# Perceiver block on one core: rounding the context of the next but one batch on ACT and DVE in place of POOL

## The reference

```python
def _L0_xattn_ref(q, k, v, mask, wq_w, wq_b, wk_w, wk_b, wv_w, wv_b, wo_w, wo_b):
    qh = _split_heads(q @ wq_w.T + wq_b)
    kh = _split_heads(k @ wk_w.T + wk_b)
    vh = _split_heads(v @ wv_w.T + wv_b)
    scores = jnp.einsum('bhqd,bhkd->bhqk', qh, kh) / jnp.sqrt(jnp.float32(D_K))
    scores = jnp.where(mask, scores, jnp.float32(-1000000000.0))
    attn = jax.nn.softmax(scores, axis=-1)
    out = jnp.einsum('bhqk,bhkd->bhqd', attn, vh)
...
x = x + _L0_xattn_ref(_layernorm(x, axis=-1), ctx_1024, ctx_1024, mask_1x1xSxS2_bf1, ...)
```

## Time and profile before

| | |
|---|---|
| median of 3 runs | 1529.22 us (1527.67 to 1531.32) |
| profiled execution: its time | 1530.81 us |
| its span in the profile | 1528.6 us, mean granted TensorE clock 0.992 |
| PE busy | 1470.1 us (96%) |
| DVE busy | 999.5 us (65%) |
| ACT busy | 921.0 us (60%) |
| POOL busy | 447.8 us (29%) |

### The profile page before, as it was taken

One profiled execution on the slowest core, in us unless ns is written; L12 is line 12 of the kernel. 1 busy time (PEld: TensorE's weight loads), 2 busy tenths in 40 slices (PEclk: granted clock), 3 DMA queues, 4 the chain that ended last, 5 costly groups with the idle time before them and its releaser, 6 DMA issues. The chain is left out here.

```text
span 1528.6 us, 56227 instructions
## 1 busy us (share of the span) xinstructions
PE 1470.1 (96%) x23420; PEld 1241.6 (81%) x23420; DVE 999.5 (65%) x3958; ACT 921.0 (60%) x1825; POOL 447.8 (29%) x564
## 2 busy tenths in 40 slices
PE   7999999999999999999999999999999987899899
PEld 4788888888888888888888888888888873566588
DVE  5766767676666776767666666676677745654345
ACT  4455666566566665666666666666666663587483
POOL 4433333333333333333333333333333302300043
PEclk9999999999999999999999999999999999799999
DMA  5644444444444444444444444444444314100012
GB/s 160 198 115 111 115 113 116 110 118 112 115 116 109 118 114 112 113 117 117 111 117 114 116 111 113 117 113 112 112 114 116 74 25 143 40 1 1 1 56 83
DMA packets 91759, 156.24 MB, mean 102 GB/s; under 512 B 44897, under 2 KB 55905, under 8 KB 91489
## 3 DMA queue, kind: packets, MB, share of 16 engines
q1 hardware_dynamic: 91216, 151.57, 36.8%
q0 software_dynamic: 288, 1.05, 0.2%
HBM read 69.61 MB, written 4.19 MB: 48 GB/s over the span
## 5 line engine op out<-in xcount | busy, mean ns | idle before, releaser
L674 DVE CUSTOM_DVE_ANT_0 junk<-bank,mask_q 128x400 bf16<-128x400 f32 (+1 forms) x1024 | 547.3, 571 | 183.9 <-issue 176.1
L620 ACT ACTIVATE probs<-bank 128x512 f32<-128x512 f32 (+1 forms) x832 | 467.8, 596 | 120.4 <-PE bank L808 111.1
L590 POOL CAST ctx_hi<-ctx_raw 128x400 fp32r<-128x400 f32 x248 | 122.7, 524 | 785.4 <-PE bank L765 785.4
L808 PE MATMUL bank<-qstack,kstack 104*128 104x128 f16 (+1 forms) x3328 | 289.3, 220 | 4.2 <-ACT probs L620 3.4
L765 PE MATMUL bank<-wv_hi,ctx_hi 128*128 128x256 f32 (+1 forms) x832 | 279.8, 336 | 0.0
L785 PE MATMUL bank<-kstack,qstack 96*128 96x400 f16 (+1 forms) x1024 | 267.2, 336 | 4.3 <-DMA qstack<-q_parts 2.2
L640 ACT ACTIVATE v<-bank 128x256 f32<-128x256 f32 (+1 forms) x416 | 159.8, 384 | 180.8 <-PE bank L765 174.6
L663 DVE SCALAR_TENSOR_TENSOR k_lo<-bank,bk,k_hi 128x400 f16<-128x400 f32 (+1 forms) x256 | 162.0, 633 | 160.6 <-ACT k_hi L630 160.5
L808 PEld LDWEIGHTS bank<-qstack,kstack 104*128 104x128 f16 (+1 forms) x3328 | 213.8, 99 | 64.6 <-issue 16.6
L630 ACT ACTIVATE k_hi<-bank,bk 128x400 f16<-128x400 f32 (+1 forms) x256 | 152.4, 595 | 175.0 <-PE bank L755 166.5
L593 POOL TENSOR_TENSOR ctx_lo<-ctx_raw,ctx_hi 128x400 fp32r<-128x400 f32 x248 | 253.8, 1045 | 0.0
(11 more groups left out here) (171 smaller groups left out, 1629.8 us busy)
## 6 DMA issues: line engine op xcount, KB each, us to landing
ctx_raw<-in_ctxT SPq DMA_DIRECT2D x32, 1602.0 KB, 6.9
kstack<-k_hi SPq DMA_DIRECT2D x512, 100.1 KB, 2.2
kstack<-k_lo SPq DMA_DIRECT2D x256, 100.1 KB, 2.2
weight<-in_w SPq DMA_DIRECT2D x18, 256.0 KB, 2.7
x<-in_xT SPq DMA_DIRECT2D x8, 512.0 KB, 8.5
qstack<-q_parts SPq DMA_DIRECT2D x192, 16.0 KB, 5.3
out_yT<-y SPq DMA_DIRECT2D x8, 256.0 KB, 3.2
weight<-in_sw SPq DMA_DIRECT2D x3, 512.0 KB, 5.9
```

Of the source, the lines that this page charges most:

```text
L590: nc.gpsimd.tensor_copy(c_hi[:, k, s0:s0 + n], raw[:, k, s0:s0 + n]).then_inc(ctx_hi, 1)
L620: nc.scalar.activation(probs[kt % NP][0:m, GROUPS * h:GROUPS * (h + 1), :], st[h][0:m, :], ACT.Exp, scale=DK ** -0.5 / (UP * UP)).then_inc ...
L674: nc.vector.tensor_tensor_reduce(junk[i % SM][:, 0:n], sm[i % SM][:, 0:n], w["mask_q"][:, s0:s0 + n], 1.0, -3.0e38, ALU.add, ALU.max, part ...
L808: mm = nc.tensor.matmul(st[h][0:m, g * PW:(g + 1) * PW], kstack[b.slot][0:KROWS, p, kt * P:kt * P + m], qstack[b.slot][0:KROWS, p, :], sta ...
```

## The change

The H steps go from POOL to ACT (the two roundings, as `ACT.Copy`) and DVE (the two subtractions). POOL has no turns any more; it still rounds batch 1 ahead of turn 0. The H's move to the ends of slots 4, 6, 9 and 12, each behind the values step that it waits for (V3, V6, V9, V12) in the order of ACT's own steps.

```diff
-    SLOTS = ["L K K S0 S1", "K K O S0 S1 K K", "S0 S1 K K M M M", "S0 S1 V P P P P M V M M M", "V S0 S1 M V",
-             "M M M V S0 M S1 M", "M V H S0 M V M M S1", "V M S0 S1 H M P P P M", "M H M S0 V S1 M", "V S0 M M M S1",
-             "V S0 M M M S1 P", "P M S0 V M M S1 G H", "S0 V S1 T P N P P"]
+    SLOTS = ["L K K S0 S1", "K K O S0 S1 K K", "S0 S1 K K M M M", "S0 S1 V P P P P M V M M M", "V S0 S1 M V H",
+             "M M M V S0 M S1 M", "M V S0 M V M M S1 H", "V M S0 S1 M P P P M", "M M S0 V S1 M", "V S0 M M M S1 H",
+             "V S0 M M M S1 P", "P M S0 V M M S1 G", "S0 V S1 T P N P P H"]
...
-        def turn(cur, nxt, ahead, third):
-            for kt in range(KT):
-                for what, i in slots[kt]:
-                    if what == "H" and ahead:
-                        split(ahead, i)
-
         def ones(_):
...
-        turns(pool, turn)
...
+        def split_hi(b, c):
+            s0, n = CHUNKS[c]
+
+            if c == 0:
+                act.wait_ge(ctx_in, 16 * (b.n + 1))
+            act.wait_ge(v_proj, KT * (b.n - 1) + -(-min(s0 + n, S2) // P))
+            for k in range(NK):
+                nc.scalar.activation(c_hi[:, k, s0:s0 + n], raw[:, k, s0:s0 + n], ACT.Copy).then_inc(ctx_hi, 1)
...
+        def split_lo(b, c):
+            s0, n = CHUNKS[c]
+            for k in range(NK):
+                dve.wait_ge(ctx_hi, SPLIT * b.n + NK * c + k + 1)
+                nc.vector.tensor_tensor(c_lo[:, k, s0:s0 + n], raw[:, k, s0:s0 + n],
+                                        c_hi[:, k, s0:s0 + n].bitcast(F32), ALU.subtract).then_inc(ctx_lo, 1)
```

More of the change, by code:

```diff
@@ L641, in values, with turn @@
                                  ACT.Copy).then_inc(v_done, 1)
-        def turn(cur, nxt, split, third):
+        def split_hi(b, c):
[5 more added lines that the diff above has]
+                nc.scalar.activation(c_hi[:, k, s0:s0 + n], raw[:, k, s0:s0 + n], ACT.Copy).then_inc(ctx_hi, 1)
+        def turn(cur, nxt, ahead, third):
             for kt in range(KT):
                 for what, i in slots[kt]:
+                    if what == "H" and ahead:
+                        split_hi(ahead, i)
                     if what == "S" and cur:
@@ L710, in outputs, with turn @@
             nc.vector.tensor_tensor(attn_out[:, :, b.n * S:(b.n + 1) * S], o_both[:], rsum[:], ALU.mult).then_inc(out_done, 1)
-        def turn(cur, nxt, split, third):
+        def split_lo(b, c):
[4 more added lines that the diff above has]
+                                        c_hi[:, k, s0:s0 + n].bitcast(F32), ALU.subtract).then_inc(ctx_lo, 1)
+        def turn(cur, nxt, ahead, third):
             for kt in range(KT):
                 for what, i in slots[kt]:
+                    if what == "H" and ahead:
+                        split_lo(ahead, i)
                     if what == "K" and nxt:
```

## The result

| | before | changed |
|---|---|---|
| median (range, runs) | 1529.88 us (1527.67 to 1531.32, 4) | 1601.27 us (1597.34 to 1603.05, 4) |
| ratio | | 1.046, interval 1.0444 to 1.0476 |
| span of the profiled execution | 1528.6 us | 1595.5 us |

What follows compares the result with a forecast made beforehand. PE was taken to bound the kernel, with about 1% idle in the loop. Terms of 49.5 + 1 + 2 + 19 = 71.5 us on a span of 1528.6 gave a predicted median of 1601 us, range 1578 to 1622.

Steps and rivals of the forecast that it cites:

- H0: Chunk 0's step: DVE waits for ACT's roundings, maxima queue behind, PE loses 1.65 us a turn, 49.5 us in all.
- Prices: Lengths of the moved work: 0.52 us for a rounding on ACT, 0.57 us for a subtraction on DVE.
- the contended 0.72: Upper bound for one DVE subtraction, from a row with POOL at work beside it; not taken, as POOL is idle.
- H1 and H2: Chunk 1's and chunk 2's steps: other work covers nearly all the delay, PE's matmuls late by 0.04 us, together 1 us.
- H3 and M0: Turn's end: context load issued 1.43 us later, the turn's first M matmul 0.76 late, 0.65 taken, 19 us.
- the 2.44: First turn's gap in us from load's landing to first M matmul, taken as minimum, small transfers landing after the load.
- K2: PE's step after `k_lo` at the turn's end: 0.05 us later a turn, 2 us in 30 turns.
- Only H0: Rival: only chunk 0's step costs, the load's delay is hidden by a larger margin; 1582 us, chance 0.17.
- All four: Rival: all four chunks' steps cost, with subtractions 0.1 us longer and a 0.9 us first-matmul wait; 1620 us, chance 0.14.
- the clock: Rival: PE's granted clock falls in the loop because PE idles each turn; over 1650 us, chance 0.03.
- Not slower: Rival: DVE finds the rounded parts ready and the maxima's slack covers the subtractions; 1529 us, chance 0.06.

Runs made afterwards that it cites:

- run 1: Changed kernel with DVE's subtractions of chunk 0 moved to the end of slot 6 and of chunk 1 to slot 7, ACT's roundings left in place: 1554.72 us.
- run 4: Changed kernel with DVE's subtractions of chunk 0 cut to 2 columns, DVE still waiting for both roundings: 1590.30 us.
- run 5: Changed kernel with DVE's subtractions of chunk 0 three maxima later, so that the roundings are ready by then: 1561.23 us.
- run 2: Changed kernel with the load of the context issued by POOL in place of SP, after the last subtraction: 1596.98 us.
- run 6: Changed kernel with the load of the context cut into four, one part per chunk, each issued by SP once its chunk is rounded: 1578.03 us.

## Why the prediction was right

**The bound.** PE had no slack in the loop, so a wait at one place came through to the end nearly undiminished: of 70.5 us that the distances show at H0 and M0, 67.3 are left over the thirty turns (see the sum).

**Prices.** The subtraction was taken as 0.57 us by two rows of which neither was the operation. It measured 0.57 (the two in 1.06, as the chunk maxima follow each other), and the rounding 0.53 for 0.52. With POOL idle the contended 0.72 did not come up.

**H0.** Forecast: 1.65 us a turn, M8 1.84 behind V3's evacuation, M11 2.51 behind it, M13 3.52. Measured in the turn above: 1.83, 2.46 and 3.48, and a mean loss of 1.62. Chunk 0 was the step that mattered and the walk named the instructions that pay. Runs 1, 4 and 5 show it from three sides.

**H1 and H2.** Forecast at 0.04 us a turn: nothing measurable, as their matmuls keep their distances within 0.01. H1's margin of 0.04 held, and H2's 0.04 of lateness did not come about.

**H3 and M0.** The load went out later by 1.41 us a turn (forecast 1.43), and M0 is 0.76 later behind T on the mean (0.76 in the walk, 0.65 taken). The size was right and the reason was not. The step "M0 cannot follow the landing closer than about 2.44: small transfers queued behind the load come in after it" fell, and with it the sentence that the 0.76 stands by the order of the queue. M0 followed the load's landing by 2.32 us on the mean and by less than 2 us in 10 of 29 turns (1.55 in the nearest), which the prediction had named as a sign of being wrong. Of the 180 query transfers issued right behind a load, 76 landed before it did. And run 2 took the load out of the queue, which by that reason should have brought back some 20 us and brought 4 or 5. What the runs showed in its place is that the first keys, issued 4.7 us behind the load on the mean, are slowed by its running at the same time (3.4 us for 2.4). The turn from which the 2.44 was taken has this in it already, in the last of its queries and the last of its first three keys:

```profile
73.66 0.45 SPq L552 DMA_DIRECT2D qstack<-q_parts  x1
DMA to landing us min/median/max: 5.4/5.4/5.4
75.35 0.58 SPq L559 DMA_DIRECT2D kstack<-k_hi  x1
DMA to landing us min/median/max: 4.5/4.5/4.5
```

The queries were there at 79.1 and the key at 79.8, and M0 ran at 79.89: it was the keys it waited for, whatever the bracket names. The estimate came out since it carried that slowness along. The queries' lateness is not nothing: they land 0.9 us ahead of M0, where it was 2.1. An estimate from the landings of the 29 turns, with the keys at 2.2 us and the queries as they are, leaves M0 0.4 of the 0.76 late. K2 runs 0.01 us later behind T, where 0.05 was forecast.

**The sum.** By the trace 1.62 in 30 turns and 0.76 in 29 are 70.5 us. Against this, about 3 us of PE's own gaps vanished (8.0 us in the earlier trace rows, 4.8 after; M2 to M3 above), which the prediction held to be constant. Together 67.3, near the 66.9 between the two spans. The forecast had 1 us too much at H0, 1 at H1 and H2 and 2 at K2, 3 too little at M0, and nothing for the gaps. The medians differ by 71.4 us, where 71.5 were forecast, and part of that is luck: the terms are off by up to 3 us each, and the two medians lie 4.5 us further apart than the profiled executions.

**The rivals.** *Only H0* is run 6, which made it true at 1578 (forecast 1582). *All four* and *the clock* did not come about. *Not slower* failed at the point it named: DVE could not have the rounded parts before V3 was evacuated.

What stays open is why exactly the keys are slow beside the load (how the 16 engines share themselves between the two); no run changed the size or the shape of the key transfers. Open too is why PE's own gaps became shorter.

## What to carry to other kernels

Work that is moved to a half idle engine is priced by what stands behind it in that engine's stream, and by what it must wait for there, not by its length: here 1 us of work, behind a wait for ACT and ahead of what PE needed, cost 1.6 us a turn, three maxima later 0.33, and nine maxima later nothing. An engine that waits on a second engine should do so behind the work that a third one is waiting for. And when a step ends later than before, look at what transfer it starts, and at what else must land while that transfer runs; splitting the big transfer so that its parts start as their space comes free took that cost away.

## What the runs showed of the hardware

Beside a load of 1.6 MB in flight, transfers of 100 KB took longer to land. The first three of a turn took 3.4 us on the mean of the changed kernel (up to 4.5), where the load was issued by SP as they were, and 3.2 us where POOL issued it (run 2); they took 2.4 us in the kernel before and 2.3 with the load in four parts (run 6). Transfers of 16 KB issued right behind the load on its queue took 5.6 us on the median, and 76 of 180 landed before the load did; issued 4.5 us ahead of it (run 2) they took 1.9, and behind a load in four parts (run 6) 2.3. A load issued by POOL took 7.3 us to land on the median, and so did one issued by SP. ACT's roundings and DVE's subtractions, both in SBUF, did not slow each other: a rounding took 0.53 us beside a subtraction and 0.54 without one, a subtraction 0.58 beside a rounding and 0.57 without one.
